# Cross-attention opening: norms on two engines, key pieces between transposes, key transfers by head group

## What is computed

```python
x = x + _L0_xattn_ref(_layernorm(x), ctx_1024, Wq, bq, Wkv, bkv, Wout, bout)   # 16 heads of 16
x = x + _L0_attn_ref(_layernorm(x), w_qkv, w_out, b_out)
x = x + _L0_ffn_ref(_layernorm(x), gate_w, w_gate, w_up, w_down, sw_gate, sw_up, sw_down)
x = x + _L1_xattn_ref(_layernorm(x), ctx_1024, W, b)                           # mean of the context
x = x + _L1_attn_ref(_layernorm(x), mask, W_qk, W_v, W_out, b_out, conv)
x = x + _L1_ffn_ref(_layernorm(x), W1, b1, W2, b2)
```

## Time and profile before

| | |
|---|---|
| median of three runs | 1322.51 us |
| profiled execution | 1335.78 us |
| its span, first to last instruction | 1334.0 us |
| mean granted TensorE clock | 0.93 |
| TensorE matmul busy | 1198.3 us (90%) |
| VectorE busy | 701.1 us (53%) |
| ScalarE busy | 563.1 us (42%) |
| GpSimd busy | 381.9 us (29%) |

### The profile page before, as it was taken

One profiled execution on the slowest core, in us unless ns is written; L12 is line 12 of the kernel. 1 busy time (PEld: TensorE's weight loads), 2 busy tenths in 40 slices (PEclk: granted clock), 3 DMA queues, 4 the chain that ended last, 5 costly groups with the idle time before them and its releaser, 6 DMA issues. The chain is left out here.

```text
span 1334.0 us, 32325 instructions
## 1 busy us (share of the span) xinstructions
PE 1198.3 (90%) x13863; PEld 1051.8 (79%) x13863; DVE 701.1 (53%) x1111; ACT 563.1 (42%) x923; POOL 381.9 (29%) x339
## 2 busy tenths in 40 slices
PE   4799999999999999999999988787696999388799
PEld 4789889889999998999998977665575777266588
DVE  6555665565575475476466443365562221554732
ACT  4455555555555555555555532225521222112400
POOL 4632332332342342243243200153153000422000
PEclk9899999999999999999999985597888999689989
DMA  6937647657556566665664550280021121315045
GB/s 196 209 85 174 152 104 164 144 123 156 133 140 140 134 149 128 144 148 120 160 147 105 123 107 1 83 332 1 1 82 72 40 64 56 110 33 209 2 173 195
DMA packets 61732, 161.47 MB, mean 121 GB/s; under 512 B 24904, under 2 KB 38296, under 8 KB 58520
## 3 DMA queue, kind: packets, MB, share of 16 engines
q1 hardware_dynamic: 58904, 154.18, 45.6%
q0 software_dynamic: 1536, 4.20, 0.9%
q10 hardware_dynamic: 1152, 1.05, 0.2%
HBM read 70.56 MB, written 9.44 MB: 60 GB/s over the span
## 5 line engine op out<-in xcount | busy, mean ns | idle before, releaser
L366 ACT ACTIVATE xa_pt<-xa_sc 128x1024 f32<-128x1024 f32 (+1 forms) x224 | 212.4, 962 | 150.7 <-PE xa_sc L558 150.7
L412 DVE TENSOR_REDUCE xa_mx<-xa_sc 128x2 f32<-128x804 f32 x256 | 243.7, 991 | 41.7 <-PE xa_sc L542 41.7
L558 PE MATMUL xa_sc<-xa_queries,xa_keys 104*128 104x128 f32 (+1 forms) x1664 | 232.5, 285 | 2.4 <-DVE xa_queries L427 1.8
L558 PEld LDWEIGHTS xa_sc<-xa_queries,xa_keys 104*128 104x128 f32 (+1 forms) x1664 | 206.6, 196 | 21.1 <-issue 8.4
L479 PE MATMUL xa_pj<-xa_ctx_hi,xa_wk 128*128 128x400 f32 (+1 forms) x512 | 157.4, 349 | 0.9 <-DVE xa_qst L440 0.9
L479 PE MATMUL xa_pj<-xa_wv,xa_ctx_hi 128*128 128x256 f32 (+1 forms) x832 | 155.3, 286 | 0.1
L542 PE MATMUL xa_sc<-xa_keys,xa_queries 96*128 96x402 f32 x512 | 139.4, 376 | 12.2 <-DMA xa_keys<-xa_kst_hi 7.1
L569 PE MATMUL xa_op<-xa_pt,xa_values 128*32 128x64 f32 x6656 | 141.1, 228 | 7.7 <-ACT xa_pt L366 3.3
L295 POOL TENSOR_TENSOR xa_ctx_lo<-xa_raw,xa_ctx_hi 128x1600 fp32r<-128x1600 f32 (+1 forms) x32 | 115.9, 3623 | 78.0 <-DVE xa_ctx_hi L405 75.4
L479 PEld LDWEIGHTS xa_pj<-xa_wv,xa_ctx_hi 128*128 128x128 f32 (+1 forms) x832 | 126.2, 185 | 8.0 <-issue 6.5
L300 POOL TENSOR_TENSOR xa_kst_lo<-xa_wk,xa_kst_hi 128x400 fp32r<-128x400 f32 x64 | 67.3, 1052 | 226.8 <-ACT xa_kst_hi L345 226.8
(11 more groups left out here) (288 smaller groups left out, 1740.8 us busy)
## 6 DMA issues: line engine op xcount, KB each, us to landing
xa_keys<-xa_kst_hi SPq DMA_DIRECT2D x256, 200.2 KB, 6.1
xa_keys<-xa_kst_lo SPq DMA_DIRECT2D x128, 200.2 KB, 5.4
xa_raw<-in_ctxT SPq DMA_DIRECT2D x15, 1601.0 KB, 8.8
gf_w<-in_gf_w SPq DMA_DIRECT2D x16, 1024.0 KB, 7.1
moe_ex<-in_moe_ex SPq DMA_DIRECT2D x8, 1088.0 KB, 15.3
xa_queries<-xa_qst SPq DMA_DIRECT2D x96, 32.0 KB, 3.5
moe_slots_in<-in_moe_zero SPq DMA_DIRECT2D x1, 2944.0 KB, 16.5
moe_xs<-moe_slots_in SPq DMA_DIRECT2D x23, 128.0 KB, 2.1
```

The costliest lines, as they stand in the source:

```text
L366: nc.scalar.activation(PT[ptslot(step)][0:rows, 0:nt], SC[bank(step)][0:rows, 0:nt], ACT.Exp, scale=float(D0) ** -0.5).then_inc(ex_done, 1)
L412: nc.vector.tensor_reduce(mx[:, u // 2, 2 * (u % 2):2 * (u % 2) + 2], SC[bank(step)][:, :, 0:MXN], AX.X, ALU.max).then_inc(mx_done, 1)
L558: last = mm(SC[bank(step)][0:rows, kk, a * P:(a + 1) * P], KS[:, 2 * a + h, kt * P:kt * P + rows], QS[b % 2][:, 2 * a + h, :], start=True, ...
```

## The change

Four edits in the opening.

Norm: VectorE normalises tiles 0 to 3, ScalarE tiles 4 to 7 as `rstd * x + shift`, with `shift = -mean * rstd` by one more VectorE operation. ScalarE's four come behind its rounding of context 0 and wv. The semaphore `norm` becomes `norm_dve` and `norm_act`, and the later norms count from one T less.

Order: the transposes become two steps `L`, the first ahead of the list, the second between `K(0,0)` piece 3 and the first `V`. `Q(0)` waits for the first copies alone; the first `mx` waits for both.

Transfers: `keys` runs over groups outside and copies inside. For batch 0, half 0, the first six transfers count on `keys_in` and the others on `kst_in[0]`; `mx` 0 waits for the first six, `mx` 4 for the others. SP issues the ones rows at once, after a wait for the landing of the zero rows, where it did so behind the second context.

Sums: the sums of context 1 leave `cv(1)` and become two steps `cs` after `st` 2 and `st` 3 of the first phase.

```diff
-    o = split(0) + K(0, 0)[:2] + [("Q", 0, 0, 0)] + K(0, 0)[2:] + V(0, 0, 4) + K(0, 1) + V(0, 4, 7) + split(1)
+    turns = [("L", 0, 0, u) for u in range(2)]
+    o = turns[:1] + split(0) + K(0, 0)[:2] + [("Q", 0, 0, 0)] + K(0, 0)[2:] + turns[1:] + V(0, 0, 4) + K(0, 1) + V(0, 4, 7) + split(1)
     for b in range(B):
         queries = {2: [("Q", b // 2 + 1, 0, 0)]} if b % 2 and b + 1 < B else {}
+        sums = {2 + u: [("cs", 1, 0, u)] for u in range(2)} if b == 0 else {}
...
-        o += xattn_phase(b, 0, K(b + 1, 0), V(b + 1, 0, 4), {1: e} | queries)
+        o += xattn_phase(b, 0, K(b + 1, 0), V(b + 1, 0, 4), {1: e} | queries | sums)
...
+        def keys_landed(eng, b, h):
+
+            if (b, h) == (0, 0):
+                eng.wait_ge(E["keys_in"], 16 * DMAS_K // 2)
+            eng.wait_ge(kst_in[h], 16 * (DMAS_K * (b + 1) - (0 if h else DMAS_K // 2)))
...
-                for r in range(3):
-                    for q in range(4):
+                for q in range(4):
+                    for r in range(3):
                         sp.dma_start(KS[32 * r:32 * r + 32, 2 * q + h, :].bitcast(f32),
-                                     kstage[h][TERMS[0][r]][32 * q:32 * q + 32].bitcast(f32)).then_inc(kst_in[h], 16)
+                                     kstage[h][TERMS[0][r]][32 * q:32 * q + 32].bitcast(f32)).then_inc(E["keys_in"] if (b, h) == (0, 0) and q < 2 else kst_in[h], 16)
...
             sp.dma_start(*constant_rows(rec, slice(96, KROWS), 0, 8)).then_inc(rows_in, 16)
+            sp.wait_ge(rows_in, 16)
+            for a in range(4):
+                sp.dma_start(*constant_rows(o_sb, slice(96 + 2 * a, 98 + 2 * a), 2 * a, 2 * a + 2)).then_inc(rows_in, 16)
...
                     sp.dma_start(raw[:, :, 0:NK], ctxT[b + 1]).then_inc(raw_in, 16)
-                    if b == 0:
-                        sp.wait_ge(rows_in, 16)
-                        for a in range(4):
-                            sp.dma_start(*constant_rows(o_sb, slice(96 + 2 * a, 98 + 2 * a), 2 * a, 2 * a + 2)).then_inc(rows_in, 16)
...
-                    pool.wait_ge(norm, T)
+                    pool.wait_ge(norm_dve, T // 2)
+                    pool.wait_ge(norm_act, T // 2)
...
-            for g in (0, 2):
-                act.wait_ge(tr, g + 1)
-                nc.scalar.activation(lnT[:, 0, (g // 2) * 512:(g // 2) * 512 + 512], LNP[g], ACT.Copy).then_inc(ev_act, 1)
-            act.wait_ge(w_in, 16 * 6)
-            act.wait_ge(wv_lo, 1)
+            act.wait_ge(shift_done, 1)
+            for t in range(T // 2, T):
+                nc.scalar.activation(y[t], X[:, t], ACT.Identity, bias=shift[:, t:t + 1], scale=rstd[:, t:t + 1]).then_inc(norm_act, 1)
             for step in order:
                 k, b, h, u = step
+                if k == "L":
+                    act.wait_ge(tr, 2 * u + 1)
+                    nc.scalar.activation(lnT[:, 0, u * 512:u * 512 + 512], LNP[2 * u], ACT.Copy).then_inc(ev_act, 1)
+                if step == ("K", 0, 0, 0):
+                    act.wait_ge(w_in, 16 * 6)
+                    act.wait_ge(wv_lo, 1)
...
-                        act.wait_ge(kst_in[h], 16 * DMAS_K * b)
+                        keys_landed(act, b - 1, h)
...
-            for t in range(T):
-                nc.vector.tensor_scalar(y[t], X[:, t], mv[:, t, 0:1], rstd[:, t:t + 1], ALU.subtract, ALU.mult).then_inc(norm, 1)
+            nc.vector.scalar_tensor_tensor(shift[:], mv[:, :, 0], -1.0, rstd[:], ALU.mult, ALU.mult).then_inc(shift_done, 1)
+            for t in range(T // 2):
+                nc.vector.tensor_scalar(y[t], X[:, t], mv[:, t, 0:1], rstd[:, t:t + 1], ALU.subtract, ALU.mult).then_inc(norm_dve, 1)
...
+                if k == "cs" or k == "cv" and b != 1:
+
+                    lo, hi = CVCOLS[u]
                     for ch in range(CH):
                         nc.vector.tensor_reduce(csum[:, ch, u, b:b + 1], raw[:, ch, lo:hi], AX.X, ALU.add).then_inc(csum_done, 1)
...
+            def turns(half):
+
+                for g in (2 * half, 2 * half + 1):
+                    for a in range(4):
+                        t = 4 * half + a
+                        pe.wait_ge(norm_act if half else norm_dve, a + 1)
+                        last = nc.tensor.transpose(LNP[g][:, a * P:(a + 1) * P], y[t][:, g % 2 * P:(g % 2 + 1) * P], c["ident"])
+                    last.then_inc(tr, 1)
...
                     if b == 0:
                         pe.wait_ge(w_in, 16 * 6)
-                        pe.wait_ge(ev_act, 2)
-                        pe.wait_ge(ev_dve, 2)
+                        pe.wait_ge(ev_act, 1)
+                        pe.wait_ge(ev_dve, 1)
...
                 elif k == "mx":
+                    if step == ("mx", 0, 0, 0):
+                        pe.wait_ge(ev_act, 2)
+                        pe.wait_ge(ev_dve, 2)
+                        pe.wait_ge(E["keys_in"], 16 * DMAS_K // 2)
+                    if u == (4 if step[:3] == ("mx", 0, 0) else 0):
+                        keys_landed(pe, b, h)
                     if u == 0:
-                        pe.wait_ge(kst_in[h], 16 * DMAS_K * (b + 1))
```

## The result

The changed kernel took 1320.21 us in the median of 20 runs, the kernel before 1323.67 in 20 runs beside it. The ratio of the two, changed over before, is 0.9978 with a 95% interval of 0.9968 to 0.9987, which is 1.7 to 4.2 us less and clear of no change. Forecast were 1318.2 us and 4.3 us less, within 1314.5 to 1322.8, and "same" (within 0.5%) as the likeliest outcome, which it is. The measured 1320.21 lies 0.2 us above the forecast's own range (1316.5 to 1320) and inside the whole one.

A forecast was written before the change was run, and what follows sets the result against it. The opening before the full cross-attention loop was taken to set the gain: -5.8 us at the next batch's first value piece, +1.5 for a clock fall, sum -4.3, from 1322.5 to 1318.2 us; own range 1316.5 to 1320, whole 1314.5 to 1322.8.

The forecast's parts named there:

- What bounds: Opening before the long cross-attention loop: TensorE is nearly full in the loop, so a microsecond gained before arrives as one.
- Normalising and the split of wv: Opening norm: VectorE's four tiles end by 12.0 us, ScalarE's by 15.2; wv's split ends near 16.2, not moving the sum.
- First key pieces: TensorE's opening: piece 0 at 15.65 us, piece 3 at 22.5 (-4.8), transposes +1.0, fill ends 3.8 us earlier at 38.9.
- Transfers: SP's queue in the opening: free at about 21.3 us, first six keys land at about 41, all at 45.8.
- What is late next: Next batch's first value piece: GpSimd's bias adds bound it, moving it from 59.23 to 53.4 us, -5.8 us.
- The clock: Idle time before the next batch's value pieces: granted clock falls, 3 us at half rate cost +1.5 us.
- Moved sums and key order: Second context's two sums (3.66 us) move to VectorE idle time, costing nothing; grouped keys cost nothing after the first phase.
- The clock stays: Rival: the idle time before the value pieces brings no clock fall; sum -5.8 us, 1316.7 us; chance 0.34.
- held twice: Rival in the opening: GpSimd holds VectorE through both subtractions, piece 3 at 26.3 us; 1321 us in all; chance 0.12.
- The key order: Rival in the loop: grouped key transfers take over 1.6 times as long, each phase waits; 1334 us at 0.5 each; chance 0.06.

The follow-up runs named there:

- the first experiment: Changed kernel with the ones rows issued behind the second context again; ratio to the kernel before 0.9981, value piece at 53.98 us instead of 56.50.
- the base: Changed kernel with ones rows behind the second context and bias adds behind the next batch's key pieces; ratio to the kernel before 0.9943, first score product at 54.91 us.
- TensorE kept busy: The first experiment plus ten needless TensorE products before the next batch's first value piece; from that piece to the transposed maxima 3.03 us instead of 4.56.

## Why the prediction was right or wrong, point by point

*What bounds.* Right: the lead at the first score product (2.61 us) was still 2.34 us at the norm ahead of the experts.

*Normalising and the split of wv.* Right. VectorE's four tiles end at 12.07, the split of wv lasts 2.13 us and ends at 16.06 (forecast 16.2), between GpSimd's two subtractions. ScalarE's four took 2.06 us, 0.5 each and not 0.3 to 0.4, and ended at 15.87 instead of 15.2; nothing waited for them.

The port rule of the Trainium skill (SBUF — State Buffer, "SBUF: two separate sides") says that a VectorE operation with two inputs in SBUF can't run beside a GpSimd operation that reads SBUF: the second to start waits. wv's split is such an operation, and the row agrees: 2.13 us here against 0.68 in the earlier trace rows, where GpSimd was idle. No term of the sum hung on it.

*First key pieces.* Right within 0.6 us. Piece 0 at 15.66 (15.65). Pieces 0 and 1 ran wholly at the slow pitch, 4.14 us and not 3.52 (with 4.0 as the forecast's bound), so the query projection started at 19.80 (19.2 to 19.7) and piece 3 at 23.05 (22.5). The eight transposes took 0.8 us (1.0). The fill ended at 38.95, as forecast (38.9).

*Transfers.* Here the prediction was wrong, in two places. SP's wait for the zero rows ended at 22.89, not at 21.3: I took the end of the flow as the landing. With four issues of the ones rows (3.23) and a slower one of the context (1.00), the queries started at 27.35 instead of 24.8. **The step that failed** is that the context had no landing in the sum. I let it be issued at 24.2 and wrote "the context, the queries and the keys; its price is in this sum", but beside the 0.6 us of its issue the context had no term. It was issued at 26.24 and landed at 39.84, 13.6 us later, with the keys on the same queues from 32.6. The first six keys landed at 45.21 and not 41, the rest by 49.5 (45.8). With the context ahead of the ones rows the first experiment has 40.08 and 45.84. Two slips in the adding don't move the sum: the last issue is at 40.0 and not 40.1, and 45.8 + 3.7 is 49.5 and not 49.8.

*What is late next.* The mechanism was right in each link: the value piece was released by ScalarE, that by GpSimd, with the bias adds before it, and moving them moved the end by 1.5 us. Mis-sized was the start of this chain. I had it move by the fill, from 41.84 to 38.0; it started at 40.98, when the context was cast. So the value piece came at 56.50 instead of 53.4, -2.7 us and not -5.8. With the context issued early the chain did start on the fill, and the value piece came at 53.98: the forecast of -5.8 was one for that kernel (-5.2 measured).

*The clock.* Its price was right, its place wrong. Behind later keys the last maximum product ended at 54.43, so the idle time was 2.07 us and not 3.6, and the clock stayed at 1.00. That the shorter idle time is the reason isn't shown. In the first experiment 2.45 us of idle time came with a fall and 1.5 us. So the forecast of -4.3 us held 3.1 us of gain that wasn't there and 1.5 us of a loss that didn't come; measured at the first score product are -2.6. The two errors partly cancel: that the time fell in the range is in part luck, and no proof of the sum.

*Moved sums and key order.* I priced the sums at nothing, and the grouped keys were in the sum only as a first product at 41. In the base the sums are worth 3.1 us and the grouped keys with their two waits 5.9. What they are worth in the changed kernel no run shows, but its rows speak against a price of nothing. VectorE casts the context without a break (5.39 us from 39.84), and GpSimd's second split starts right behind the last cast; 1.9 us of sums between the casts would have moved the chain that releases the value piece. And with all twelve keys awaited, the first maximum product could start at 49.5 only. The maxima took 9.2 us (45.21 to 54.43), so they would have ended at 58.7, behind the 56.50 of the value piece. By these estimates each part was worth some 2 us there.

*The rivals.* "The clock stays" came true in the clock, with later keys as the rival's own remark has it, but not in its sum of -5.8 us. VectorE wasn't held twice in the changed kernel; it was where it normalised all eight tiles (7.95 us for four). The key order slowed nothing: the lead held through the loop.

## What to carry to other kernels

When a wait is put on a queue, write down a landing for every transfer behind it, not only for those that the change is about, and follow each landing to its first reader. Where an edit removes a hole, look for the chain of small jobs on the next engine (here eight bias adds that nobody needed for a long time) and move them out of the order before the steps that others wait for; two late steps in one chain hide each other, so mending one alone shows a small part of what both bring. Measure the opening by a landmark in the trace, since 2 us in 1320 lie at the edge of what a timing can show, and find out first how far that landmark moves when nothing was changed.

## What the runs showed of the hardware

An operation of VectorE that was waiting got in between two subtractions that GpSimd had back to back: wv's split ended at 16.06, and GpSimd's second one ended at 19.56. The tile of the earlier trace rows had done the same.

The length of one idle time didn't tell whether the clock falls. It fell around 2.45 us (first experiment), 2.18 us (sums behind the casts) and 2.96 and 2.15 us (VectorE alone on the norm, ahead of key piece 3 and of the first key piece of batch 1). It stayed at 1.00 around 2.07 us (changed kernel), 2.09 us (all transposes first) and 2.36 us (TensorE kept busy, ahead of its first maximum product). And in the first experiment it also fell before 45 us, where no idle time since the fill was longer than 1 us. A fall cost 1.5 us of TensorE's work in the first experiment.

The transfer of the zero rows moved at 50 GB/s, and SP went on some 1.6 us after the end that I had read from the flow. The transfer of the second context took 7.5 us from issue to landing before the change and 7.2 in the first experiment, but 13.6 in the changed kernel, behind the ones rows and with queries and keys beside it. The key transfers ran at about 205 GB/s in both orders: 204 in the stretch from 49.84 in the earlier trace rows, 205 from 54 to 57 us in the changed kernel.
